# A weight tile loaded earlier, stacks loaded in parts, and unused products of the identity

## The reference, cut to what matters

```python
x = x + xattn(layernorm(x), ctx, ctx, w_q, w_k, w_v, w_out, mask)     # 32 heads of 32, 8 key/value groups, 1024 keys
x = x + ffn(layernorm(x))        # x @ W_base.T + b + low-rank update through an inverse real FFT
x = x + fake_quant(layernorm(x)) @ fake_quant(ctx)                    # 0..255 codes
x = x + streams(x)               # four streams of 256, Sinkhorn with 50 iterations
```

## Time and profile before

| | us |
|---|---|
| median of 3 runs | 1101.72 |
| lowest, highest | 1100.82, 1101.84 |
| profiled execution, its own time | 1102.68 |
| its span, first to last instruction | 1100.9 |
| TensorE matmul busy | 1040.5 (95%) |
| VectorE busy | 844.3 (77%) |
| ScalarE busy | 663.4 (60%) |
| granted TensorE clock, mean | 0.978 of full speed |

### The profile page before, as it was taken

One profiled execution on the slowest core, in us unless ns is written; L12 is line 12 of the kernel. 1 busy time (PEld: TensorE's weight loads), 2 busy tenths in 40 slices (PEclk: granted clock), 3 DMA queues, 4 the chain that ended last, 5 costly groups with the idle time before them and its releaser, 6 DMA issues. The chain is left out here.

```text
span 1100.9 us, 21010 instructions
## 1 busy us (share of the span) xinstructions
PE 1040.5 (95%) x7578; PEld 784.9 (71%) x7578; DVE 844.3 (77%) x1876; ACT 663.4 (60%) x1126; POOL 77.1 (7%) x68
## 2 busy tenths in 40 slices
PE   6999998899999999999999999998999999969948
PEld 5878887677777777777777777775788887536527
DVE  5764544599999999999999999964674343879998
ACT  4332220398899888888988888942222114647607
POOL 1211012200000000000000000000003212310000
PEclk9999999899999999999999999999899999989969
DMA  8458779840232232113332311165424000000003
GB/s 334 163 184 284 252 247 265 291 131 20 60 74 71 67 71 67 40 41 71 71 71 67 71 51 37 40 229 199 127 84 166 0 0 1 1 1 1 1 0 153
DMA packets 55568, 112.96 MB, mean 103 GB/s; under 512 B 7724, under 2 KB 21164, under 8 KB 55388
## 3 DMA queue, kind: packets, MB, share of 16 engines
q1 hardware_dynamic: 55452, 112.26, 32.7%
q0 software_dynamic: 64, 0.00, 0.0%
HBM read 83.99 MB, written 27.26 MB: 101 GB/s over the span
## 5 line engine op out<-in xcount | busy, mean ns | idle before, releaser
L876 DVE CUSTOM_DVE_ANT_0 XS<-b_psS,b_mbias 128x1024 f32<-128x1024 f32 x256 | 311.0, 1215 | 0.9 <-PE b_psS L755 0.7
L831 ACT ACTIVATE XS<-XS,b_mins 128x1024 f32<-128x1024 f32 x256 | 295.9, 1156 | 11.0 <-DVE b_mins L876 10.4
L791 PEld LDWEIGHTS b_psT<-ident,XS 128*128 128x128 f32 x2048 | 230.6, 141 | 68.7 <-issue 50.5
L791 PE MATMUL b_psT<-ident,XS 128*128 128x128 f32 x2048 | 274.2, 277 | 1.3 <-ACT b_PT L839 1.3
L885 DVE COPY b_PT<-b_psT 128x512 f32<-128x512 f32 x256 | 176.9, 691 | 34.7 <-PE b_psT L791 33.1
L839 ACT COPY b_PT<-b_psT 128x512 f32<-128x512 f32 x256 | 149.5, 584 | 46.4 <-PE b_psT L791 38.2
L755 PE MATMUL b_psS<-XTh 128*128 128x512 f32 x512 | 156.8, 424 | 3.7 <-DVE b_mins L876 1.9
L769 PE MATMUL b_psO<-b_PT,XTh 128*32 128x256 f32 x1984 | 132.8, 385 | 0.0
L755 PEld LDWEIGHTS b_psS<-XTh 128*128 128x128 f32 x512 | 85.5, 190 | 22.4 <-DVE b_mins L876 10.2
L769 PEld LDWEIGHTS b_psO<-b_PT,XTh 128*32 128x32 f32 x1984 | 51.7, 109 | 42.1 <-issue 20.8
L406 ACT ACTIVATE a_oh<-a_psM 128x512 fp32r<-128x512 f32 x24 | 14.2, 596 | 84.2 <-PE a_psM L329 50.8
(11 more groups left out here) (261 smaller groups left out, 1570.7 us busy)
## 6 DMA issues: line engine op xcount, KB each, us to landing
XS<-in_ctx SPq DMA_DIRECT2D x16, 512.0 KB, 5.8
XTh<-QHd SPq DMA_DIRECT2D x32, 256.0 KB, 4.7
XTh<-QLd SPq DMA_DIRECT2D x32, 256.0 KB, 5.3
XS<-in_ctx_turned SPq DMA_DIRECT2D x8, 512.0 KB, 10.9
XS<-in_x SPq DMA_DIRECT2D x8, 512.0 KB, 10.4
a_wst<-in_L_xattn_w_q SPq DMA_DIRECT2D x8, 512.0 KB, 5.7
a_xn<-in_ctx_turned SPq DMA_DIRECT2D x8, 512.0 KB, 4.1
QHd<-a_oh SPq DMA_DIRECT2D x16, 256.0 KB, 5.6
```

What stands on the lines that cost most here:

```text
L791: last_t = pe.transpose(psT[:, kt, :], Pr[:, k % PR, kt * P:(kt + 1) * P], ident[:])
L831: act.activation(Pr[:, k % PR, :], Sc[:, k % 4, :], ACT.Exp, bias=mins[:, k % 4:k % 4 + 1], scale=-1.0, accum_out=sums[:, u, j:j + 1]).the ...
L876: dve.tensor_tensor_reduce(out=Sc[:, k % 4, :], in0=psS[:, k % 2, :], in1=mbias[:, qt, :], scale=1.0, scalar=3.4e38, op0=ALU.add, op1=ALU.min,
```

## The change

Three things. The load of weight tile 14 is issued before the attention loads. The six parts of the stacks are loaded in three steps: E's three parts when E is split, T's two high parts when the high rows are there, T's low part from ScalarE's queue when the low rows are there; VectorE still waits for all six. And TensorE gets plain float32 products of the identity with itself, whose result nobody reads: 20 before `first_keys`, 14 after the last product of stage A (into the bank of product 28), and 9 after the first two scores of attention.

```diff
--- before.py
+++ after.py
@@ -63,6 +63,12 @@
                        pattern=[[-1, P]], channel_multiplier=1).then_inc(done, 1)
 
 
+
+
+def keep_warm(pe, bank, ident, count):
+
+    for _ in range(count):
+        pe.matmul(bank, ident[:], ident[:], start=True, stop=True)
 
 
 class Handover:
@@ -272,6 +278,7 @@
                 store(M_Q + 2 * t)
                 store_q2(t)
                 store(M_Q + 2 * t + 1)
+            load_w(NW - 2)
             sp.wait_ge(mm_done, M_V1)
             for u in range(2):
                 sp.wait_ge(stored[u], 32 * (KVT + KT))
@@ -279,7 +286,6 @@
             for u in range(2):
                 hand.load_scores(sp, QHd, QLd, KHd, KLd, u, u)
                 hand.load_values(sp, Vd, u, u)
-            load_w(NW - 2)
             for c in range(KT, 2 * KT):
                 m = M_V1 + c - KT
                 if c + 2 < 2 * KT:
@@ -352,6 +358,8 @@
                                                start=False, stop=(k == KT - 1 and a is WTl))
                     mm.then_inc(mm_done, 2)
 
+            pe.wait_ge(setup, 2)
+            keep_warm(pe, psM[:, 3, 0:P], ident, 20)
             first_keys()
             pe.wait_ge(setup, 3)
             for i in range(4):
@@ -373,6 +381,8 @@
                     turn_v(2)
                 elif m == M_K1:
                     turn_v(3)
+            pe.wait_ge(mm_free, 2 * NW - 4 + 1 + 4)
+            keep_warm(pe, psM[:, 0, 0:P], ident, 14)
 
         @block.scalar
         def _(act):
@@ -811,6 +821,7 @@
 
             score(0, 0)
             score(0, 1)
+            keep_warm(pe, psO[:, 1, 0:P], ident, 9)
             body(0, first=True)
             with pe.Fori(1, BG // 2 - 1) as it:
                 body(it)
@@ -1183,6 +1194,9 @@
         def slot(t):
             return slice(t % QT * P, (t % QT + 1) * P)
 
+        def stack_rows(r):
+            return slice(r * RANK, (r + 1) * RANK)
+
         def row_tile(weights, t):
             return weights[:, ds(t, 1), :].rearrange("p a n -> p (a n)")
 
@@ -1205,11 +1219,14 @@
             sp.dma_start(XR[:, 1:NT, :], x[P:TOK, :].rearrange("(t p) n -> p t n", p=P)).then_inc(x_in[1], 16)
             sp.wait_ge(op_split, 2)
             early.load_attention(sp, AOd, 3)
-            sp.wait_ge(T_split, 1)
-            for r, (t_rows, e_rows) in enumerate(((hi_rows, hi_rows), (lo_rows, hi_rows), (hi_rows, lo_rows))):
-                rows = slice(r * RANK, (r + 1) * RANK)
-                sp.dma_start(TS[rows, :].bitcast(F32), t_rows[0:RANK, 0, :].bitcast(F32)).then_inc(stacks_in, 16)
-                sp.dma_start(ES[rows, :].bitcast(F32), e_rows[0:RANK, 1, :].bitcast(F32)).then_inc(stacks_in, 16)
+            sp.wait_ge(low, 7)
+            for r, e_rows in enumerate((hi_rows, hi_rows, lo_rows)):
+                sp.dma_start(ES[stack_rows(r), :].bitcast(F32), e_rows[0:RANK, 1, :].bitcast(F32)
+                             ).then_inc(stacks_in, 16)
+            sp.wait_ge(T_step, 3)
+            for r in (0, 2):
+                sp.dma_start(TS[stack_rows(r), :].bitcast(F32), hi_rows[0:RANK, 0, :].bitcast(F32)
+                             ).then_inc(stacks_in, 16)
 
             def load_base(t):
                 if t + 2 < NT:
@@ -1479,6 +1496,9 @@
                                        ACT.Copy, scale=UPDATE_SCALE).then_inc(T_step, 1)
                     act.wait_ge(T_step, 2)
                     act.activation(hi_rows[0:RANK, 0, :], T32, ACT.Copy).then_inc(T_step, 1)
+                    act.wait_ge(T_split, 1)
+                    act.dma_start(TS[stack_rows(1), :].bitcast(F32), lo_rows[0:RANK, 0, :].bitcast(F32)
+                                  ).then_inc(stacks_in, 16)
                 if i in MID:
                     weights_hi(MID[i])
             act.wait_ge(op_split, NT)
```

## The result

| | before | after |
|---|---|---|
| median of 4 runs each, us | 1101.7 | 1091.05 |
| lowest, highest | 1100.82, 1101.84 | 1089.52, 1091.83 |
| profiled execution, its own time | 1102.68 | 1089.52 |
| its span | 1100.9 | 1087.7 |
| granted TensorE clock, mean | 0.978 | 0.986 |

The ratio is 0.9898, 95% interval 0.9877 to 0.9919. The forecast was 1088.2 with a range of 1085.0 to 1093.5: the time lies in it, 2.9 us above the forecast. The profiled execution was forecast at 1089.2 and took 1089.52, but that closeness is the sum of errors of both signs.

The account below looks back on a forecast made before the run. TensorE bounds the projections, TensorE and VectorE attention, in a chain where gains at four TensorE waits carry through. 5.2 - 0.2 + 1.4 + 0.1 + 7.0 = 13.5 us gives 1089.2 profiled, median 1088.2, range 1085.0 to 1093.5.

Parts of the forecast that it names:

- The weight tile: Hole near 179 us in the projections: with tile 14's load moved, wait and half-rate matmuls both go, gaining 5.2 us.
- The new last tile: Weight tile after the moved one: POOL starts 1.3 us sooner, otherwise 0.1 lost; rival that it becomes the wait, chance 0.05.
- one each 0.112 us: Price of one unused fp32 product on TensorE, from a row of 16 in 1.95 us; 0.22 at the lower clock level.
- Fourteen: Unused products at the end of the projections: end at 208.5 against VectorE's 208.32, cost 0.2 us; 2.3 without overlap.
- Nine: Unused products after attention's first two scores: 1.2 us in a 1.95 us gap, costing nothing; opening gains 1.4 with clock held.
- Twenty: Unused products at the start: end by 6.0 us, before the first tile at 8.33; no delay, gain 0.1 us.
- the start pays: Rival at the start: the clock comes up during the twenty and stays, 1.2 us more, 1087.0; chance 0.08.
- The stacks: Hole at 766.8 us before the update: earlier stack loads leave a 1.0 us hole and no lower clock, gaining 7.0 us.
- the row of the same transfer: Profile row of the last stack DMA before the change: VectorE reads the stack 5.05 us after issue; basis for the 7.0.
- a sign of being wrong: At the stacks: a stack part landing over 6 us after its issue would show the prediction wrong.
- The argument against contention: At the stacks: the last stack DMA took 5.05 us even with two attention tiles issued just behind it.
- the contention rival: At the stacks: last T part lands at 768.5 to 770, clock falls; gain 3.3 instead of 7.0, 1091.9; chance 0.12.

## Why the prediction was right, point by point

**The weight tile: right in place and size.** 5.2 forecast, 5.25 found, and the tile waits for its place rather than for its load, as said. The new last tile is early by more than was worked out: POOL starts 4.0 us sooner, 1.9 without the earlier start, where 1.3 was forecast. What the prediction did not see is that the next store is late instead: KLd holds ScalarE's last operation up to 2.3 us behind the last product, and up to 1.4 in the traces with the fourteen, which cover it there.

**The unused products: the step that failed is "one each 0.112 us".** The row it was read from the earlier trace rows counts 16 instructions in 1.95 us, and I took an instruction for a product. A float32 product is two instructions, as the 40 and the 28 rows of the new kernel show, so it costs 0.235 us at the upper level. The kernel could have told: at line 1912 it makes 8 products for each token tile, and the row counts 16. Each term that used the price moved:
- Fourteen were to end at VectorE's end and cost 0.2; they end 1.4 us behind it, and the stage's end comes 1.73 us later (3.58 - 1.85). The prediction named the case as wrong if the unused products set the stage's end by more than 0.5 us, and priced it (2.3).
- Nine were to take 1.2 and take 2.17 us, in a gap that has room for them; the opening is 1.32 us shorter (1.4 forecast).
- Twenty were to end at 6.0 and leave 2.3 us of stillness ahead of the first tile; they end at 8.6, with the tile's arrival. So there is no first stillness, and the clock is up for the first tile. It stays up behind the second one in five of the nine traces with the twenty and nothing in the gap. That is 2.06 us in this trace, against 0.1 in the sum and a rival, the start pays, of 1.2 more at a chance of 0.08. The kernel without them is slower by 0.0032 of the ratio, about 3.5 us, with intervals that overlap, and by 1.0 to 2.8 us by the estimate on its own chip. So the rival came true in about half the executions seen, through an error in my own price, and how much of it is in the median is not settled.

**The stacks: right mechanism, one term too small.** The landing was taken at 5.05 us, from the row of the same transfer; it was 6.56, and alone it is 4.1. The prediction named over 6 us as a sign of being wrong, and it was met. The argument against contention, that in the kernel before two tiles stood right behind it as well, did not carry: there the part stood in front of them on SP's queue, where each issue takes its time (1.16 us for the last part), so they came over a microsecond later; from ScalarE's queue it has no such lead. (Why it took 5.05 there and 4.1 to 4.2 with the tiles out of the way is not shown; five other parts were issued just ahead of it.) Half of the contention rival is true in all nine traces with the part on ScalarE's queue and the tiles not held: the part is late, by 2.5 us in the profiled execution. The other half, that the clock falls, is true in two of nine. Those two gained 3.1 and 3.8 us at the stacks, which is the rival's price (3.3); the profiled execution, with 6.28, was not one of them.

**The total.** 2.0 too little at the start, 1.6 too much at the passage, 0.7 too much at the stacks: 0.3 us apart in the profiled execution. The median is 2.9 above the forecast of it. The profiled execution was the lowest of its four, 1.53 below their median, and I had taken off the 0.96 us by which the one before stood above its median: together 2.5 of the 2.9. Good cases came together in that execution, at the start (32.56 in a range of 32.5 to 35.6) and at the stacks (52.61 in a range of 52.6 to 55.8). That the time fell into the range rests on the tile and the stacks; that the sum came within 0.3 us of the span is luck.

**Two terms lean on each other.** With the tile late again and a slow start (35.56), TensorE came to the hole 1 us later, the load landed where it did before, and the clock was not lost: the hole cost 2.8 us and not 5.25. In that trace the hole gave part of the slow start back. With the hole gone, the whole of the start's gain reaches the end of attention: the stretch to the last product is 166.92 or 166.93 us in all twelve such traces, whatever the start.

## What to carry to other kernels

Count products and instructions separately before pricing one by the other: a row's count is of instructions, and one of the same call in the new place settles it. Filling a stand still on TensorE pays if the filler ends before the wait does; what sticks out is paid unless something else is later still, and at a stage's end half as many held the clock as well. Where a small transfer is waited for, hold back the large ones that nobody wants yet, or issue it ahead of them; a queue of its own did not shield it. And look at several traces of a wait before trusting its size: one execution showed 1.57 us and the clock kept, others 2.2 to 2.4 us and the clock lost.

## What the hardware showed that was not expected

- Stillness of 1.99 us ahead of six matmuls left the clock up in one execution and 2.05 us let it fall in another, in kernels with the same code there. In the hole at 179 us it was 2.52 us idle (kept) and 3.36 (fell, 0.50 in 183 to 185). In front of the stacks 2.23 and 2.28 us kept it, 2.21 and 2.44 lost it. Before attention's opening it fell after 1.7 us, four matmuls, and less than 1.95 us more. The level after a stand still is not settled by its length alone.
- The forty instructions of the twenty products took 7.09 us in the changed kernel's trace, 7.43 in its repeat, and 6.26 to 7.68 over the eleven traces that have them: the clock came up at different times. The Trainium skill (TensorE: Matmul & The Clock Gate, Part 1: The HAM clock gate) says that the place where the clock turns at the start differs between runs of the same kernel; these traces agree.
- A 160 KB copy from SBUF to SBUF took 4.1 us to land with no larger load issued behind it, and 6.1 to 6.8 us in nine traces with 1 MB issued 0.3 us later from another engine.
